# Summing the squares of the keys: one fp32 matmul, or two bf16 matmuls fed by GpSimd, in the first cross attention of a two-layer decoder

## The reference, cut to what matters

```
q = (hidden @ Wq).reshape(B, Sq, H, D);  k = (ctx @ Wk)...;  v = (ctx @ Wv)...
q = q * rsqrt(mean(q*q, -1) + 1e-5) * gq
k = k * rsqrt(mean(k*k, -1) + 1e-5) * gk
attn = softmax(einsum('bqhd,bkhd->bhqk', q, k) / sqrt(D));  out = (attn @ v) @ Wo
```

## Time and profile before

| | before |
|---|---|
| median of 3 runs | 2655.49 us (2650.91 to 2658.3) |
| the profiled execution | 2651.95 us, of which the span is 2650.2 us |
| PE busy over the span | 2442.6 us, 92% |
| DVE busy | 1849.5 us, 70% |
| ACT busy | 1590.4 us, 60% |
| POOL busy | 720.4 us, 27% |

### The profile page before, as it was taken

How to read it: one execution, slowest core, us unless ns; L and a number is a source line. 1 busy time by engine, 2 the same in 40 slices (tenths; PEclk the granted TensorE clock), 3 DMA queues, 4 the chain that set the end, 5 groups by cost and what they waited for, 6 DMA issues and landing times. The chain is left out here.

```text
span 2650.2 us, 57668 instructions
## 1 busy us (share of the span) xinstructions
PE 2442.6 (92%) x21584; PEld 1567.2 (59%) x21584; DVE 1849.5 (70%) x3371; ACT 1590.4 (60%) x2718; POOL 720.4 (27%) x671
## 2 busy tenths in 40 slices
PE   7999998989999999999678999999999999999964
PEld 4565555446666666665345666665466666665432
DVE  5777777557777777775556666668487888884597
ACT  5767775158777878884133555664177777774242
POOL 5666665601110011012233222225200000012211
PEclk9999999999999999999888999999999999999987
DMA  3333335225666666666340444446178777776400
GB/s 95 88 77 82 89 75 132 90 57 106 118 115 118 106 110 116 117 110 136 107 167 1 93 93 93 95 91 148 19 140 147 143 146 149 148 147 129 106 1 32
DMA packets 769428, 273.83 MB, mean 103 GB/s; under 512 B 737904, under 2 KB 740720, under 8 KB 767600
## 3 DMA queue, kind: packets, MB, share of 16 engines
q1 hardware_dynamic: 767504, 265.82, 48.0%
q0 software_dynamic: 1760, 5.77, 0.7%
HBM read 84.55 MB, written 6.44 MB: 34 GB/s over the span
## 5 line engine op out<-in xcount | busy, mean ns | idle before, releaser
L875 ACT ACTIVATE phl<-p,ri 128x1024 bf16<-128x1024 f32 (+4 forms) x512 | 437.3, 854 | 413.3 <-DVE ri L1184 387.4
L1194 DVE SCALAR_TENSOR_TENSOR phl<-p,ri,phl 128x1024 bf16<-128x1024 f32 (+4 forms) x512 | 511.7, 999 | 103.3 <-issue 75.1
L886 ACT ACTIVATE p<-p,nb 128x1024 f32<-128x1024 f32 (+4 forms) x512 | 435.8, 851 | 54.2 <-DVE nb L1177 39.8
L1255 PE MATMUL ps<-wo_lo,v_hi 128*128 128x128 bf16 x2496 | 439.3, 219 | 0.0
L1254 PE MATMUL ps<-wo_hi,v_hi 128*128 128x128 bf16 x2240 | 395.8, 219 | 23.2 <-DMA wo_hi<-phl 16.0
L1256 PE MATMUL ps<-wo_hi,v_lo 128*128 128x128 bf16 x2240 | 395.6, 219 | 0.0
L1254 PE MATMUL ps<-k_hi,q_hi 128*128 128x512 bf16 (+3 forms) x768 | 272.7, 355 | 22.3 <-DVE nb L1175 20.1
L1255 PE MATMUL ps<-k_lo,q_hi 128*128 128x512 bf16 (+3 forms) x768 | 272.2, 354 | 0.0
L1256 PE MATMUL ps<-k_hi,q_lo 128*128 128x512 bf16 (+3 forms) x768 | 271.9, 354 | 0.0
L1255 PEld LDWEIGHTS ps<-wo_lo,v_hi 128*128 128x128 bf16 x2496 | 244.9, 98 | 33.2 <-issue 0.3
L1254 PEld LDWEIGHTS ps<-wo_hi,v_hi 128*128 128x128 bf16 x2240 | 219.3, 98 | 68.7 <-DMA wo_hi<-phl 28.1
(11 more groups left out here) (197 smaller groups left out, 6140.0 us busy)
## 6 DMA issues: line engine op xcount, KB each, us to landing
raw_kv<-in_wkvself SPq DMA_DIRECT2D x32, 512.0 KB, 3.7
raw_q<-in_wqself SPq DMA_DIRECT2D x32, 256.0 KB, 2.6
raw_q<-in_woself SPq DMA_DIRECT2D x32, 256.0 KB, 2.9
raw_q<-in_wqcross SPq DMA_DIRECT2D x32, 256.0 KB, 2.9
raw_q<-in_wocross SPq DMA_DIRECT2D x32, 256.0 KB, 3.0
wo_hi<-phl SPq DMA_TRANSPOSE x384, 3.2
wo_lo<-phl SPq DMA_TRANSPOSE x384, 3.1
raw_kv<-in_wkvcross SPq DMA_DIRECT2D x24, 256.0 KB, 3.2
```

The costliest lines, as they stand in the source:

```text
L875: nc.scalar.activation(m["ph"](qt, w), m["p"][:, qt % 2, 0:w], ACT.Copy, scale=ri[:, qt % 2:qt % 2 + 1]).then_inc(p_norm, 1)
L886: nc.scalar.activation(prob, prob, ACT.Exp, scale=1.0 if L.rms else -1.0, bias=nb[:, qt % 2:qt % 2 + 1], accum_out=rs[:, qt % 2:qt % 2 + 1 ...
L1194: nc.vector.scalar_tensor_tensor(out=m["pl"](qt, w), in0=m["p"][:, qt % 2, 0:w], scalar=ri[:, qt % 2:qt % 2 + 1], in1=m["ph"](qt, w), op0= ...
L1255: nc.tensor.matmul(o, l(0), r(1), start=False, stop=False)
```

## The change

Four things are edited.

1. The order of the jobs: quarter 1 is K1, KN0 and quarter 2 is Q, KN1; each sum now comes behind the projection, not ahead of it. PE, ACT and DVE all walk the same list.
2. KN: PE waits for `sq_lo` and does two bf16 matmuls with a bf16 matrix of ones (`onesb`, made once at the start), one on the hi half of the squares, one on the lo half.
3. GpSimd: `squares` makes these halves, `sqh` by a copy and `sql` by a subtraction, for each K job. It waits for ACT's squares, and for the KN matmul that read the halves before. It stands ahead of the query norms and the weight pieces of its quarter.
4. ACT: before it writes new squares of a K or Q job it waits until GpSimd has split the last ones.

```diff
-            plan = [[("K", 0)], [("KN", 0), ("K", 1)], [("KN", 1), ("Q", 0)], [("QN", 0), ("V", 0), ("V", 1)]]
+            plan = [[("K", 0)], [("K", 1), ("KN", 0)], [("Q", 0), ("KN", 1)], [("QN", 0), ("V", 0), ("V", 1)]]
...
+            nc.gpsimd.tensor_scalar(onesb[:, :], ones[:, :], 1.0, 1.0, ALU.mult, ALU.mult).then_inc(onesb_ok, 1)
...
+                def squares(n, it, qt, jobs):
+                    for kind, half in jobs:
+                        if kind == "K":
+                            pool.wait_ge(sq_ok, at(lambda n: 3 * (n + 1) + half + 1, n, it))
+                            if half:
+                                pool.wait_ge(job_mm, at(lambda n: c["job"] + L.before(n, 1) + 2, n, it))
+                            elif n >= 0:
+                                pool.wait_ge(job_mm, at(lambda n: c["job"] + L.before(n - 1, 2) + 2, n, it))
+                            nc.gpsimd.tensor_scalar(m["sqh"][:, :], m["sq"][:, :], 1.0, 1.0, ALU.mult, ALU.mult).then_inc(sq_hi, 1)
+                            pool.wait_ge(sq_hi, at(lambda n: 2 * (n + 1) + half + 1, n, it))
+                            nc.gpsimd.tensor_tensor(m["sql"][:, :], m["sq"][:, :], m["sqh"][:, :], ALU.subtract).then_inc(sq_lo, 1)
...
+                            squares(n, it, qt, L.jobs(n, qt))
                             query_norms(n, it, qt, L.jobs(n, qt))
...
                             if L.rms:
+                                kept_squares = 2 * u + (2 if kind == "Q" else half)
+                                if kept_squares:
+                                    act.wait_ge(sq_lo, kept_squares)
                                 nc.scalar.activation(m["sq"][:, :], bank, ACT.Square).then_inc(sq_ok, 1)
...
                     elif kind == "KN":
-                        pe.wait_ge(sq_ok, at(lambda n: c["sq"] + 3 * (n + 1) + half + 1, n, it))
-                        last = nc.tensor.matmul(bank, ones[:, :], m["sq"][:, :], start=True, stop=True)
+                        pe.wait_ge(onesb_ok, 1)
+                        pe.wait_ge(sq_lo, at(lambda n: 2 * (n + 1) + half + 1, n, it))
+                        nc.tensor.matmul(bank, onesb[:, :], m["sqh"][:, :], start=True, stop=False)
+                        last = nc.tensor.matmul(bank, onesb[:, :], m["sql"][:, :], start=False, stop=True)
```

More of the change, by code:

```diff
@@ L149, in build @@
         ones = sb("ones", [P, P], F32)
+        onesb = sb("onesb", [P, P], BF16)
         idx = sb("idx", [P, IT], I32)
@@ L185, in build @@
         fg_mm, fu_mm, g_ok, u_ok, fs_ok, fy_ok = (sem(x) for x in ("fg_mm", "fu_mm", "g_ok", "u_ok", "fs_ok", "fy_ok"))
-        idb_ok = sem("idb_ok")
+        idb_ok, onesb_ok = sem("idb_ok"), sem("onesb_ok")
+        sq_hi, sq_lo = sem("sq_hi"), sem("sq_lo")
         row_in = [sem(f"row_in{i}") for i in range(11)]
@@ L300, in build @@
                 m["sq"] = sb("sq", [P, S], F32, s)
+                m["sqh"], m["sql"] = sb("sqh", [P, S], BF16, s), sb("sql", [P, S], BF16, s)
                 m["rk"] = sb("rk", [P, 2, SC], F32, s)
@@ L692, in _ @@
                         if L.rms:
+                            squares(n, None, qt, L.jobs(n, qt))
                             query_norms(n, None, qt, L.jobs(n, qt))
```

## The result

| | before | after |
|---|---|---|
| median | 2656.52 us (2650.91 to 2658.3, 4 runs) | 2679.4 us (2676.64 to 2685.7, 4 runs) |
| profiled execution | 2651.95 us, span 2650.2 | 2680.94 us, span 2679.1 |

What follows compares the result with a forecast made beforehand. The ring of ACT and DVE, not PE, bounds: 22.02 - 21.19 = +0.83 us in 31 units, +25.7, plus 0.9 in the first, together +27 on the median 2655.49: 2682 us; range 2661 to 2695.

Steps and rivals of the forecast that it cites:

- The ring, 22.02 us: Closed loop of handoffs in a unit: ACT exponential, squares, hi; DVE lo, reciprocal, scores; ACT again; forecast 22.02 us.
- The four steps: Times between ACT's `nb` rows, one a quarter, in a unit; before 4.61, 4.62, 5.83, 6.13 us, forecast 4.61, 5.22, 6.96, 5.23.
- `rk` of KN0, +0.60: Quarter 1 on DVE: `rk` now stands behind `k_lo` of K1, adding 0.60 us to step two.
- `rk` of KN1, +1.13: Quarter 2: `rk` stands on DVE behind `q_lo`, ACT's logarithm waits for it; step three 6.96 us where it was 5.83.
- the reserve: What the ring of before, about 19.9 us, had in hand under PE's unit of 21.19: 1.3 us.
- PE's 0.43 a sum: On PE, two bf16 matmuls replace an fp32 sum of 0.86 us: less by 0.43, two sums a unit.
- PE's waits, 1.9 in all: PE will idle about 1.9 us a unit, about 1 for GpSimd at KN0, about 1 for `k_lo` at Q.
- GpSimd covered, reserve 1.2 us: POOL's splits of the squares ahead of KN0 have 1.2 us in hand, so GpSimd's 114 us cost nothing.
- No contention of DVE and POOL: DVE's remainder, even at 1.50 us, is over before POOL's splits begin, 1.96 us after `nb`, so the shared port costs nothing.
- The first unit, +0.9 over the others: First unit of the loop: PE has no backlog, so it pays 0.60 + 1.13 in full, +0.9 us more.
- The clock: PE's granted clock should not suffer: it was 1.00 at 91% busy, and 20.08 of 22.02 is 91% too.
- The rival that PE gives its time back: PE stays the bound and its saved sum time returns: 28 to 34 us faster, 2621 to 2628 us; chance 0.09.

## Why the prediction was right, point by point

- *The ring, 22.02 us.* It is 21.87. The four steps were forecast as 4.61, 5.22, 6.96, 5.23 and are 4.61, 5.21, 6.90, 5.15. The two small misses are pieces that I took too long. The row for V's hi in the earlier trace rows, 1.24 us long, had waited for PE; in the changed kernel it takes 1.06, and the step over V is 0.08 shorter. The stretch from the logarithm to `nb` is 3.09 us, not 3.13. 0.15 us in 31 units is 4.6 us too much. That the median lies only 2.6 under the forecast is in part luck: 1.0 us that I didn't see (below), and a median of before that rose by 1.0 with its fourth run, went the other way.
- *`rk` of KN0, +0.60.* Step two grew by 0.60. Shown by its own experiment: the step is 5.21 wherever quarter 1 has the new order.
- *`rk` of KN1, +1.13, and what the reserve pays.* ACT's wait was forecast as about 1.5 and is 1.36; step three grew by 1.06. The run with quarter 2 alone has the same step three and pays 0.09 a unit: 0.97 of the 1.06 came out of step four, which had that much slack.
- *PE's 0.43 a sum brings nothing.* Shown twice: the order alone, with PE 0.86 us a unit busier, has the changed kernel's unit; the sums alone gave 0.17. This holds for these two orders of work; with `weigh` moved the same 0.86 gave 0.97 (21.04 to 20.07).
- *PE's waits, 1.9 in all, "about 1 at KN0 and about 1 at Q".* 0.90 and 0.88. PE's busy share fell to 93%, not to 91%: its ends are modelled, as the prediction says, and part of each wait counts as busy.
- *DVE's waits for PE ahead of the scores nearly gone.* 8.8 us in 26 waits of at most 0.3 from 600 to 1200 us, where it was 48.2 in 57.
- *GpSimd covered, reserve 1.2 us.* Covered, reserve about 1.0.
- *No contention of DVE and POOL.* Half wrong, without a price in time. The splits of the squares do keep clear of the remainder, but they push POOL's weight splits into it: the remainder at 724.77 takes 1.89 us beside the weight splits at 723.31 and 724.43, and the mean of all 110 from 600 to 1200 us is 1375 ns (count, busy us and mean in the row). Before, in the same window, none of them took more than 1.29. I had looked at the new instructions only, not at the ones they move.

```profile
L1215 DVE SCALAR_TENSOR_TENSOR phl<-p,ri,phl 128x1024 bf16<-128x1024 f32 x110 | 151.3, 1375 | 56.0 <-issue 45.0
```

  It costs nothing since DVE still waits 0.48 us for `q_hi` behind it, and 1.08 in the units where the remainder takes 1.28; both kinds of unit last 21.87.
- *The first unit, +0.9 over the others.* +1.6 where the others have +0.69: +0.9.
- *What the prediction did not see:* the 1.0 us in the last unit. Its third `phl` waits 1.30 us for a transposing DMA (0.33 before). With the order alone it waits 1.15 there, so this comes with the order and not with GpSimd's work. Why the DMA lands later was not tried.
- *The clock.* Held at 1.00, as read from the earlier trace rows. The prediction took this from a busy share of 91% over a long stretch. With 1.9 us more on one of the waits it fell in two units of three, and the mean granted clock from 600 to 1200 us was 0.95.

*The rival that PE gives its time back* was wrong for a reason that its own remedy shows: the way over the banks, 21.02 us, lay only 0.17 under the unit of 21.19, and `weigh` moved from behind the jobs to ahead of them in two quarters opens it. PE's time then comes back until the ring stops it at 20.0. The Trainium skill (Perfetto Trace Analysis, Identifying the Most-Contended Engine) names the engine with the highest occupancy as the one to optimise, with a warning about PE's busy share. Here 99.5% and a wait in every unit went together.

Left open: an order on ACT with hi ahead of the squares would shorten the ring by some 0.5 us at each of three places (an estimate, from the 0.49 between the squares and `q_hi` in the earlier trace rows). It was not tried, since DVE would then read the PSUM bank for lo while ACT still reads it for the squares. The Trainium skill (PSUM — Partial Sum Buffer, PSUM bank collisions raise a hardware error) says that two engines which access one bank at the same time raise a hardware error; no run here shows it. Left open too is an order in which GpSimd's exact halves are as fast as ACT's rounded squares.

## What to carry to other kernels

An engine that is 99% busy may still be one of several closed ways of nearly the same length; sum each ring of handoffs from the rows (here 19.9 for the ring and 21.0 for the way over the banks, beside a unit of 21.2) before counting on time taken from that engine. Work that seems to cost an engine time may be covering a wait: ask what the next instruction waits for, and put other work there first, then make the cheap version. And a job list that is walked by several engines moves all of them: the loss came from two 0.68 us instructions on DVE that nobody meant to touch.

## What the runs showed of the hardware

- An fp32 matmul of 128 x 128 by 512 columns held PE 0.86 us (716.39 to 717.25), four times the 0.22 of a bf16 one.
- PE went to half its clock behind a wait of 2.54 us in a stage in which it was otherwise busy (starts 0.37 and more apart, granted clock 0.72 over 6 us). That made 0.9 us of lateness into 2.5. It doesn't always follow: with both splits doubled it came behind 20 of 29 such waits, and other waits of 2.54 us left the clock at 1.00. With the subtraction alone doubled none of the 31 waits, 1.72 to 2.91 us long, brought it down.
- The remainder on DVE (two SBUF inputs) took up to 1.90 us in place of 1.28 beside POOL's subtractions, and 2.20 in the run with both splits doubled; POOL's own subtraction stayed at 1.16 there. The Trainium skill (SBUF — State Buffer, SBUF: two separate sides) has a lock between such an instruction and one of GpSimd that reads SBUF, held by the one that starts first for its whole length. The rows agree in the order and nearly in the size: the remainder that began 0.34 us behind POOL's subtraction (724.77 behind 724.43) overlapped it by 0.81 us and took 0.61 more.
